# Score operands copied in 2 KB pieces, and an earlier first load, in a pipelined transformer kernel

## The reference, cut to what matters

```
x = x + gate * (softmax(q k^T * scale) v @ W_proj + b)      # self attention, 16 heads of 16
x = x + softmax(q_c k_c^T * scale) v_c @ W_cproj + b        # cross attention over 77 context rows
x = x + gate * (gelu(norm(x) @ W_mlp1 + b) @ W_mlp2 + b)
```

## Time and profile before

| | |
|---|---|
| median of 3 runs | 3118.23 us (3109.76 to 3124.80) |
| the profiled execution's own time | 3119.53 us |
| its span, first to last instruction | 3117.5 us |
| mean granted TensorE clock | 0.96 |
| busy: PE, PEld, DVE, ACT, POOL | 95%, 74%, 52%, 49%, 21% |
| first load of x in `blocks` | 683.32 us |

### The profile page before, as it was taken

The page is one execution under the profiler, slowest core; times in us unless marked ns, Lnnn a source line. Parts: engine busy times, 40 slices in busy tenths (PEclk is TensorE's granted clock), DMA queues, the critical chain, the costliest instruction groups (busy, mean ns, idle before and its releaser), DMA issues.

```text
span 3117.5 us, 58368 instructions
## 1 busy us (share of the span) xinstructions
PE 2963.0 (95%) x21972; PEld 2312.7 (74%) x21972; DVE 1621.6 (52%) x3345; ACT 1528.5 (49%) x2677; POOL 652.7 (21%) x733
## 2 busy tenths in 40 slices
PE   5999999966999999999999999999999999999997
PEld 4999999964667777777777767777777776776765
DVE  1444444434656656565655555556555555555541
ACT  2444444413455555555555545555555554555552
POOL 2333333320112212211211121112211111111111
PEclk7999999987899999999999999999999999999998
DMA  4111100004353543435345454353443544435421
GB/s 136 33 44 47 32 24 24 16 25 88 81 124 90 105 94 82 106 71 102 86 95 112 85 106 94 91 122 88 105 98 83 105 91 85 108 75 102 96 56 32
DMA packets 339527, 252.36 MB, mean 81 GB/s; under 512 B 126064, under 2 KB 328672, under 8 KB 339248
## 3 DMA queue, kind: packets, MB, share of 16 engines
q1 hardware_dynamic: 336016, 243.51, 35.5%
q10 hardware_dynamic: 3232, 5.12, 0.5%
HBM read 86.45 MB, written 16.97 MB: 33 GB/s over the span
## 4 chain that ended last, share of the span: by engine, by line
PE 46%; SPq 15%; issue 7%; DMA 6%; POOL 2%; DVE 2%; ACT 1%; POOLq 0%; DVEq 0%; ACTq 0%
PE gbank L2038 9%; SPq L1167 9%; PE gbank L1900 5%; PE obank L1970 5%; PE obank L1900 4%; PE score L1936 4%; DMA qc_cat<-qc_hl 4%; PE obank L1907 3%; PE gbank L1985 3%; PE obank L2016 3%; PE gbank L1907 2%; SPq L1176 2%; PE gbank L1894 2%; PE score L1999 2%; PE score L1950 2%
## 5 line engine op out<-in xcount | busy, mean ns | idle before, releaser
L1481 ACT ACTIVATE p_f<-score 128x1024 f32<-128x1024 f32 (+1 forms) x576 | 562.5, 1020 | 442.2 <-PE score L1950 336.3
L1682 DVE TENSOR_REDUCE m_a<-score 128x4 f32<-128x1024 f32 x384 | 460.0, 1220 | 198.2 <-PE score L1936 197.2
L2038 PE MATMUL gbank<-w,h_c 128*128 128x256 f32 x1536 | 438.1, 417 | 0.9 <-ACT h_c L1498 0.9
L2038 PEld LDWEIGHTS gbank<-w,h_c 128*128 128x128 f32 x1536 | 280.5, 200 | 59.7 <-issue 2.0
L902 PE MATMUL m_ps<-m_comb,m_w 128*128 128x256 f32 x2304 | 300.6, 286 | 0.0
L902 PEld LDWEIGHTS m_ps<-m_comb,m_w 128*128 128x128 f32 x2304 | 284.9, 190 | 3.1 <-issue 1.7
L1692 DVE TENSOR_REDUCE m_b<-gbank 128x4 f32<-128x308 f32 x192 | 92.2, 480 | 338.7 <-PE obank L1985 250.0
L585 ACT ACTIVATE m_hf<-m_ps,tab 128x256 f32<-128x256 f32 x192 | 80.7, 471 | 264.1 <-PE m_ps L902 264.1
L536 POOL TENSOR_TENSOR m_hhl<-m_hf,m_hhl 128x512 fp32r<-128x512 f32 x96 | 125.3, 1305 | 397.3 <-DVE m_hhl L741 397.3
L1970 PE MATMUL obank<-p_f,v_s 128*32 128x256 f32 x3072 | 204.5, 397 | 0.0
L1936 PE MATMUL score<-k_cat,q_cat 48*128 48x256 f32 x1536 | 176.7, 326 | 28.8 <-DMA k_cat<-k_hl 12.1
(11 more groups left out here) (226 smaller groups left out, 5286.4 us busy)
## 6 DMA issues: line engine op xcount, KB each, us to landing
k_cat<-k_hl SPq DMA_DIRECT2D x288, 128.0 KB, 3.2
q_cat<-q_hl SPq DMA_DIRECT2D x288, 128.0 KB, 4.2
qc_cat<-qc_hl SPq DMA_DIRECT2D x288, 128.0 KB, 3.6
x_a<-x_after_L SPq DMA_DIRECT2D x48, 256.0 KB, 2.8
res_a<-x_after_L SPq DMA_DIRECT2D x48, 256.0 KB, 4.8
kc_cat<-kc_hl SPq DMA_DIRECT2D x288, 38.5 KB, 2.0
x_after_L<-y_c SPq DMA_DIRECT2D x32, 256.0 KB, 2.2
bias_a<-rows_L SPq DMA_DIRECT2D x48, 128.0 KB, 4.6
```

The lines of the kernel that those rows point to most:

```text
L1481: e.activation(p_f[i % 4][0:n, :], score[i % 2].ap[0:n, :, :].rearrange("p h n -> p (h n)"), ACT.Exp, scale=SCALE).then_inc(ex.sem, 1)
L1682: e.tensor_reduce(m_a[:, :, i::NPAIR].rearrange("p t h -> p h t"), score[i % 2].ap[:, :, :].rearrange("p h (t k) -> p h t k", t=TT), AX.X, ...
L2038: mm = e.matmul(B_DOWN.ap[:, tt, :], h_c[:, k, tt * P:(tt + 1) * P], weights_of(d)["w2"][:, k, :], start=(k == 0), stop=(k == MC - 1))
```

## The change

Heads h and 8 + h were in the lower and the upper 64 rows of pair h. Now pair 2j + c holds heads 8c + 2j (lower rows) and 8c + 2j + 1 (upper rows). So the lower rows take the even partitions of a source and the upper rows the odd ones, and both chunks of a partition go side by side: a copy moves 64 partitions with one run of 512 tokens (2 KB) to 16 partitions with 4 such runs. The number of copies and their bytes stay. `kc_hl` gets a 78th column (zero) per chunk, so that its runs are whole (624 bytes). The heads' numbers in the value matmuls and the permutation of the output projections follow.

SP waits for no constant before its loop; the fill of both `k_cat` and of `kc_cat` goes from DVE at the start of `blocks` to POOL at the end of its iteration 1, and SP waits for it before the first key rows. DVE copies `sel` at the end of its iteration 1, and PE waits for it in the first `recips_spread`.

```diff
-        ... kc_hl = ... sb("kc_hl", [P, 2, CC, NC_TOK], F32R)
+        ... kc_hl = ... sb("kc_hl", [P, 2, CC, CPAD], F32R)
@@ block.sync
+            def copy_rows(dst, width, src, part, i, signal):
+                for hf in range(2):
+                    at = 64 * hf + i
+                    e.dma_start(dst[at:at + QROWS:3, :, 0:width].bitcast(F32).rearrange("d (j c) n -> d j (c n)", c=CC),
+                                src[hf::2, part, :, 0:width].bitcast(F32)).then_inc(signal.sem, 16)
             def high_rows(u, dst, width, src, high, order, signal):
                 e.wait_ge(*high.at(u))
                 for i in range(3):
-                    for c in range(CC):
-                        at = 64 * c + i
-                        if order[i] == 0:
-                            e.dma_start(dst[at:at + QROWS:3, :, 0:width].bitcast(F32),
-                                        src[:, 0, c, :].bitcast(F32)).then_inc(signal.sem, 16)
+                    if order[i] == 0:
+                        copy_rows(dst, width, src, 0, i, signal)
...
             def key_rows_high(q):
+                if q == 0:
+                    e.wait_ge(s_ones, 1)
...
             def cross_key_rows_high(a):
                 if a:
                     e.wait_ge(*S["B_stp"].at(a - 1))
-                high_rows(a, kc_cat, NC_TOK, kc_hl, S["K_kh"], (0, 0, 1), S["K_kcat"])
+                else:
+                    e.wait_ge(s_one, 2)
+                high_rows(a, kc_cat, CPAD, kc_hl, S["K_kh"], (0, 0, 1), S["K_kcat"])
...
-            e.wait_ge(s_one, 2)
             for n in range(N_ITER):
@@ block.gpsimd, end of the iteration
+                if n == 1:
+                    for i in range(2):
+                        e.memset(k_cat[i][:, :, :].bitcast(F32), -1.0)
+                    e.memset(kc_cat[:, :, :].bitcast(F32), -1.0).then_inc(s_ones, 1)
@@ block.vector
-            for i in range(2):
-                e.memset(k_cat[i][:, :, :].bitcast(F32), -1.0)
-            e.memset(kc_cat[:, :, :].bitcast(F32), -1.0)
             e.memset(v_s[:, :, :, :].rearrange("p t h c -> p (t h c)"), 0.0)
             e.memset(vc_s[:, :, :].rearrange("p h c -> p (h c)"), 0.0).then_inc(s_one, 1)
-            e.wait_ge(s_one, 1)
+            e.memset(kc_hl[:, :, :, NC_TOK:CPAD].bitcast(F32), 0.0).then_inc(s_one, 1)
+            e.wait_ge(s_one, 2)
             e.memset(v_s[:, :, :, HD:HD + 1], 1.0)
-            e.memset(vc_s[:, :, HD:HD + 1], 1.0).then_inc(s_one, 1)
-            e.wait_ge(s_sel, 5)
-            e.tensor_copy(sel[:, :, :].rearrange("s c m -> s (c m)"), p_f[0][0:64, 0:2 * P]).then_inc(s_sel, 1)
+            e.memset(vc_s[:, :, HD:HD + 1], 1.0)
...
                 queries_low(q)
+                if n == 1:
+                    e.wait_ge(s_sel, 5)
+                    e.tensor_copy(sel[:, :, :].rearrange("s c m -> s (c m)"), p_f[0][0:64, 0:2 * P]).then_inc(s_sel, 1)
@@ block.tensor
             def recips_spread(u, bank, at, sent, on, done):
                 e.wait_ge(*sent.at(u))
+                if u == 0:
+                    e.wait_ge(s_sel, 6)
...
-                            mm = e.matmul(bank.ap[32 * g:32 * g + 32, i % 2, :], v_s[:, kc, 8 * hf + 2 * i + j, :],
+                            mm = e.matmul(bank.ap[32 * g:32 * g + 32, i % 2, :], v_s[:, kc, 8 * j + 2 * i + hf, :],
...
-            e.wait_ge(s_one, 2)
-            e.wait_ge(s_sel, 6)
             for n in range(N_ITER):
```

More of the change, by code:

```diff
@@ L1087, in blocks @@
         ctx, ctxT = sb("ctx", [NC_TOK, 1, D]), sb("ctxT", [P, CC, NC_TOK])
-        qc_hl, kc_hl = sb("qc_hl", [P, 2, CC, NT], F32R), sb("kc_hl", [P, 2, CC, NC_TOK], F32R)
+        qc_hl, kc_hl = sb("qc_hl", [P, 2, CC, NT], F32R), sb("kc_hl", [P, 2, CC, CPAD], F32R)
         vc_s = sb("vc_s", [NC_TOK, NH, VW])
@@ L1108, in blocks @@
         B_UP, B_RA, B_RB, B_KMT, B_DOWN, B_KP = (g0, o0, g0, o1), g1, g0, g0, g1, (g0, o1)
-        s_one, s_sel = nc.alloc_semaphore("b_const"), nc.alloc_semaphore("b_sel")
+        s_one, s_ones, s_sel = (nc.alloc_semaphore(k) for k in ("b_zeros", "b_ones", "b_sel"))
         S = signals(nc, "b",
@@ L1172, in low_rows @@
                 for i in range(3):
[L1173 to L1177, removed]
+                    if order[i] == 1:
+                        copy_rows(dst, width, src, 1, i, signal)
             def max_out(u, mT, part, dst, ready, row):
@@ L1279, in cross_key_rows_high @@
                     e.wait_ge(*S["B_stp"].at(a - 1))
-                high_rows(a, kc_cat, NC_TOK, kc_hl, S["K_kh"], (0, 0, 1), S["K_kcat"])
+                else:
+                    e.wait_ge(s_one, 2)
+                high_rows(a, kc_cat, CPAD, kc_hl, S["K_kh"], (0, 0, 1), S["K_kcat"])
             def cross_key_rows_low(a):
                 if live(a):
-                    low_rows(a, kc_cat, NC_TOK, kc_hl, S["K_kl"], (0, 0, 1), S["K_kcat"])
+                    low_rows(a, kc_cat, CPAD, kc_hl, S["K_kl"], (0, 0, 1), S["K_kcat"])
             def cross_query_rows_high(a):
@@ L1470, in high_part @@
                 for m in range(CC):
-                    ac = e.activation(dst[:, 0, m, :], view(m), ACT.Identity,
+                    ac = e.activation(dst[:, 0, m, 0:view(m).shape[1]], view(m), ACT.Identity,
                                       bias=weights_of(u)["bcol"][:, at + m:at + m + 1])
@@ L1653, in low_part @@
                 for m in range(CC):
-                    lo = e.scalar_tensor_tensor(dst[:, 1, m, :], view(m), weights_of(u)["bcol"][:, at + m:at + m + 1],
-                                                dst[:, 0, m, :].bitcast(F32), ALU.add, ALU.subtract)
+                    n = view(m).shape[1]
+                    lo = e.scalar_tensor_tensor(dst[:, 1, m, 0:n], view(m), weights_of(u)["bcol"][:, at + m:at + m + 1],
+                                                dst[:, 0, m, 0:n].bitcast(F32), ALU.add, ALU.subtract)
                 lo.then_inc(done.sem, 1)
@@ L2015, in cross_values @@
                         g, at = 2 * hf + j, hf * 512 + j * NT
-                        mm = e.matmul(bank.ap[32 * g:32 * g + 32, i % 2, :], vc_s[:, 8 * hf + 2 * i + j, :],
+                        mm = e.matmul(bank.ap[32 * g:32 * g + 32, i % 2, :], vc_s[:, 8 * j + 2 * i + hf, :],
                                       p_f[i % 4][0:NC_TOK, at:at + NT], start=True, stop=True)
@@ L2247 @@
         if name in HEAD_ROWS:
-            a = np.ascontiguousarray(a.reshape(2, 2, 2, 2, HD, D).transpose(1, 0, 3, 2, 4, 5).reshape(D, D))
+            a = np.ascontiguousarray(a.reshape(2, 2, 2, 2, HD, D).transpose(1, 3, 0, 2, 4, 5).reshape(D, D))
         arrays[f"in_{name}_dram"] = a
```

## The result

The changed kernel takes 3071.61 us (median of 6 runs, 3066.42 to 3080.66), the kernel before 3113.99 us on the same chip (6 runs, 3089.10 to 3125.17). The ratio is 0.987, with a 95% interval of 0.983 to 0.991: faster by 1.3%. A ratio here is formed from the single executions, without those that took over 1.5% longer than the fastest of their kernel, so it is not quite the quotient of the medians. The forecast was 3080 us. The profiled execution took 3075.49 us with a span of 3073.4, so 44 us less than the profiled one of before.

A forecast was written before the change was run, and what follows sets the result against it. PE nearly full, with SP's copies up to the last `qc_cat` landing nearly as long. Start 5, waits 13, clock 21 and pipeline filling 1.5 make 40.5 us off 3119.5: forecast 3080 us, range 3060 to 3117.

The forecast's parts named there:

- The bound: Whole iteration: PE busy 95% of the span, with SP's copies up to the last `qc_cat` landing nearly as long.
- The issue: SP's issue of each copy: 0.60 us whatever the pieces' count and size, so a change of 0.
- The landing: Last `qc_cat` copy of a burst: lands 0.5 us earlier with 2 KB pieces, bounds 0.2 and 0.9 us.
- The sum for the waits: PE's 34 waits on `qc_cat` at the first `cross_plain`: 0.38 us off each on average, 13 us.
- my own lower case: Whole kernel with a 0.2 us earlier landing: waits give 6 us, clock losses 11 us, time 3097 us.
- The clock: Slow iterations partly at 1.2 GHz: four of six return to full clock, 5.3 us each, 21 us.
- The reason that I gave: First `cross_plain`: `qc_cat` waits of 1.26 to 1.34 us drop the clock; 1.08 us and less mostly do not.
- The start: Start of `blocks`: load of x goes out 6.8 us earlier, 1.8 us lost to POOL's fills, leaving 5 us.
- That the pieces don't matter: Copies' landings: stay at 4.1 us, only the first load gains, 3114.5 us; chance 0.24.
- The crowding rival: Destinations of the copies: larger pieces crowd worse, last `qc_cat` copy lands 0.4 us later, 3157 us; chance 0.12.
- the cheap issue: SP's issues: 0.38 us each, all `qc_cat` waits and four slow iterations go, 3066 us; chance 0.06.
- One sign that I had named: PE's waits on `qc_cat`: under 15 us in total if the forecast is right.

The follow-up runs named there:

- the start alone: The kernel before with only the new fills, waits and `sel` copy at the start of `blocks`; 3114.4 us, ratio 0.998.
- new heads with old pieces: The changed kernel with two unused columns behind each chunk of q, k and qc, so runs are 1 KB again; 3134.4 us, ratio 1.003.
- the pieces alone: The changed kernel with the old start of `blocks` (DVE fills everything first, SP and PE wait); 3070.7 us, ratio 0.984.
- the later fills: The changed kernel, but POOL fills `k_cat` and `kc_cat` only after DVE has normalized unit 0's `x_a`; 3069.3 us, ratio 0.986.
- the last four kernels: `down` 3 to 7 moved up: changed kernel 3079.5 us; kernel before 3094.8; changed with fills after normalization 3077.6; that with `mlp_normed` ahead of `mlp_gated` 3036.5.

## Why the prediction was right, point by point

**The bound** was read rightly: PE nearly full, and SP's chain up to the last `qc_cat` landing nearly as long. The experiments add that both sides are steep: 0.2 us of earlier landing came with 1.3%, and 0.64 us of issue cost more than that.

**The issue** stayed at 0.60 us, as taken (medians for `qc_cat` 600 ns before, 596 after).

**The landing** is the term that was mis-sized. Taken was 0.5 us, "midway"; measured is 0.21 us, at the lower bound of 0.2. The argument for the middle, that a small relief would take the backlog away, failed: the share stays above 1 in the burst shown, and over all bursts it went only from 1.02 to 0.94. A piece of 2 KB came out at 112 ns, not 121.

The sum for the waits, 13 us, met 10.9 us in the profiled executions, although the landing moved by less than half of what I took. The 34 waits of the trace, each cut by 0.21 us or to nothing, give 7 us. (Cut by 0.5 us they give 14.6; my average of 0.38 us was too low, 0.43 is right.) The waits have not merely shrunk, they have gone from 34 to 21 in number. Nor are they all: of the 0.46 us that an ordinary iteration got shorter, PE's idle time ahead of `cross_plain` is 0.26. Another 0.11 is idle time ahead of the first `self_plain`, which the profile puts down to "issue" and `q_cat`, but which ends some 90 ns behind the landing of a `k_cat` copy each time but one: 10.6 us between 930 and 2900 us before, 7.2 after. Outside the filling, the prediction had no term for that wait. The remaining 0.09 I can't assign.

So it is partly luck that the total came so near. For a landing 0.2 us earlier my own lower case gave 3097 us, and 3072 was measured. I took too much for the landing and too little for what a landing is worth, and the two errors cancelled. That waits and clock both give way when the pieces grow was right; how much a tenth of a microsecond brings, the prediction had no means to say.

**The clock** gave back 16 us in the slow iterations of the profiled pair, where I had 21. It isn't the chance of one execution: between 920 and 2900 us the three profiled kernels with 1 KB pieces and PE's old order have 7, 7 and 8 half-clock iterations (before, the start alone, new heads with old pieces), and the three with 2 KB pieces have 3, none and 2 (after, the pieces alone, the later fills). The reason that I gave is only half right, and I misread one row. I had said that one slow iteration has no wait at its `cross_plain`. It has the longest of all:

```profile
2620.14 0.30 PE L1985 MATMUL gbank<-kc_cat,qc_cat 48*128 48x78 f32 x1 [2.18 <-DMA qc_cat<-qc_hl]
```

So five of the six begin with a wait of 1.26 us or more, which speaks for the reason. Against it as a limit: in the changed kernel one iteration fell behind a wait of 1.00 us while two with 1.04 us did not, and with the wait covered seven fell without any. What the traces show is a fall in the stretch from the wait through the `cross_plain` steps, behind a wait for `qc_cat` or, with `down(d, 3)` moved, without one. With the wait covered and a `down` step kept between the short matmuls, as in the last four kernels, no iteration fell in mid-span.

**The start** gave 2.7 us; predicted were 5. The load went out 6.9 us earlier (6.8 predicted), and the loss to the fills was 3.75 us where I took 1.8: the first tile waited for all three memsets and the second came behind it, which is a little over my upper bound of 3.5. The fills themselves took 4.1 us (4.7 at most), with cover for the key rows.

**The rivals.** That the pieces don't matter is excluded by the pair of the pieces alone and the new heads with old pieces, 0.984 and 1.003. What the Trainium skill says on descriptors within SBUF ("DMA: Bandwidth & Descriptors", "Why small descriptors are slow (HBM only)"), that they don't suffer from being small, holds for the size of the effect, 0.2 us in 3.4, and not for what it was worth here. It is not quite so of the packets either: 2 KB cost 112 ns in one piece and 120 in two. The crowding rival did not occur; the cheap issue did not either. One sign that I had named was missed by little: the waits on `qc_cat` are 15.8 us, not under 15.

## What to carry to other kernels

Where two paths through an iteration are within a per cent of each other, a tenth of a microsecond in a landing can be worth several times itself (here 0.21 us in 42 iterations, 9 us, came with 35): price the wait that ends last and what the clock does behind it, not the transfer. When such a wait is covered by moving work, look at what the moved work stood between: here it had kept short matmuls apart, and hidden a slow pair of DVE tiles. Look, too, at what a DVE operation runs beside: a `TENSOR_SCALAR` from SBUF to SBUF that took 0.4 us alone lost 0.97 us beside a GpSimd sum that DVE itself had just released, and putting it ahead of that release brought 1.3% here.

## What the runs showed of the hardware

The exclusion between the two engines was stronger than a share: one 0.4 us `TENSOR_SCALAR` tile took 4.17 us at the worst beside three POOL memsets in a row, so it did not get its turn between two memsets. Line 1654 of the changed kernel, ns min/median/max:

```profile
L1654 DVE TENSOR_SCALAR x_a<-x_a,p_mv,p_rstd x96: 395/408/4165, 683.7 to 2886.9; 128x256 f32<-128x256 f32 x96
```

DVE's own first memset of `k_cat`, all of it beside POOL's selects, took the same 1.76 us in the kernel before as the second, which hardly met them; so not every pair of operations excludes each other. And an issue of SP takes 0.57 to 0.60 us for these copies within SBUF, whether they move 4 KB (573 ns at the median) or 128 KB in pieces of 1 or 2 KB (600 and 596 ns).
